# A transformer block's three step lists in another order: maxima bunched, weight tests spread over the first batch, next tokens fetched at other places

## The reference

```
qkv = x @ Wqkv + bqkv                     # 256 -> 768, 16 heads of 16
att = softmax(where(causal, q @ k^T / 4, -inf))
x   = layernorm(x + (att @ v) @ Wout + bout)
h   = silu(x @ W1^T * s1) * (x @ W2^T * s2)   # 256 -> 1024
h   = gelu(h @ H1^T * sh1)                    # 1024 -> 1024, exact gelu
h   = gelu(h @ H2^T * sh2)                    # 1024 -> 1024
out = layernorm(x + h @ W3^T * s3)            # 1024 -> 256
```

## Time and profile before

| | |
|---|---|
| median of 3 runs | 2191.09 us (2189.73 to 2191.16) |
| profiled execution | 2188.74 us, span 2187.0 us |
| TensorE (PE) | 2129.8 us busy, 97% |
| VectorE (DVE) | 1248.7 us, 57% |
| ScalarE (ACT) | 1317.0 us, 60% |
| GpSimd (POOL) | 489.7 us, 22% |
| mean granted TensorE clock | 0.990 |
| first 140 us | iteration 0 (first `max` at 16.5 us, weight flag at 140.7 us) |

### The profile page before, as it was taken

The page is one execution under the profiler, slowest core; times in us unless marked ns, Lnnn a source line. Parts: engine busy times, 40 slices in busy tenths (PEclk is TensorE's granted clock), DMA queues, the critical chain, the costliest instruction groups (busy, mean ns, idle before and its releaser), DMA issues.

```text
span 2187.0 us, 52042 instructions
## 1 busy us (share of the span) xinstructions
PE 2129.8 (97%) x16294; PEld 1873.9 (86%) x16294; DVE 1248.7 (57%) x3928; ACT 1317.0 (60%) x2807; POOL 489.7 (22%) x899
## 2 busy tenths in 40 slices
...
DMA packets 95941, 167.71 MB, mean 77 GB/s; under 512 B 19204, under 2 KB 38404, under 8 KB 95672
## 3 DMA queue, kind: packets, MB, share of 16 engines
...
...
## 4 chain that ended last, share of the span: by engine, by line
PE 88%; issue 1%; ACT 1%; SPq 1%; DVE 1%; DMA 1%; POOL 0%; ACTq 0%; DVEq 0%; POOLq 0%
PE ring L1236 44%; PE ring L1221 11%; PE pM L1111 7%; PE pS L1099 6%; PE pO L1159 6%; PE ring L1249 5%; PE ring L1171 4%; PE ring L1201 2%; PE ring L1191 2%; ACT probs_a L766 1%; PE ring L1143 1%; SPq L606 0%; DMA Qs<-nm 0%; PE ring L1210 0%; DMA rec<-rec_d 0%
## 5 line engine op out<-in xcount | busy, mean ns | idle before, releaser
L916 DVE CUSTOM_DVE_ANT_0 pM<-pM,mask 128x512 f32<-128x512 f32 (+3 forms) x1024 | 497.8, 502 | 361.6 <-PE pM L1111 298.9
L1236 PE MATMUL ring<-Yhi,H 128*128 128x256 f32 x1984 | 501.8, 290 | 0.3 <-DVE c L932 0.3
L1236 PE MATMUL ring<-Xhi,H 128*128 128x256 f32 x1984 | 497.7, 289 | 0.0
L1236 PE MATMUL ring<-Ylo,H 128*128 128x256 f32 x1984 | 487.4, 282 | 0.0
L1236 PE MATMUL ring<-Xlo,H 128*128 128x256 f32 x1984 | 486.1, 282 | 0.0
L1236 PEld LDWEIGHTS ring<-Yhi,H 128*128 128x128 f32 x1984 | 377.1, 190 | 10.6 <-issue 6.5
L1236 PEld LDWEIGHTS ring<-Ylo,H 128*128 128x128 f32 x1984 | 378.0, 190 | 6.8 <-issue 3.3
L1236 PEld LDWEIGHTS ring<-Xlo,H 128*128 128x128 f32 x1984 | 379.3, 191 | 1.4
L1236 PEld LDWEIGHTS ring<-Xhi,H 128*128 128x128 f32 x1984 | 378.4, 191 | 1.5 <-issue 0.2
L1111 PE MATMUL pM<-Ks,Qs 128*128 128x512 f32 x992 | 301.1, 343 | 16.1 <-DVE mx L916 9.4
L860 ACT ACTIVATE Yhi<-ring,cols 128x256 fp32r<-128x256 f32 x248 | 117.1, 472 | 277.3 <-PE ring L1236 155.8
...
## 6 DMA issues: line engine op xcount, KB each, us to landing
qk_d<-c SPq DMA_DIRECT2D x120, 256.0 KB, 3.4
Qs<-qk_d SPq DMA_DIRECT2D x120, 192.0 KB
Ks<-qk_d SPq DMA_DIRECT2D x120, 192.0 KB
qk_d<-c SPq DMA_DIRECT2D x120, 128.0 KB, 3.1
...
raw<-in_h ACTq DMA_DIRECT2D x8, 1024.0 KB, 11.4
H<-raw ACTq DMA_DIRECT2D x8, 1024.0 KB, 10.0
```

Source lines behind the costliest of these rows:

```text
L916: nc.vector.tensor_tensor_reduce(pM[:, h % 2, 0:n], pM[:, h % 2, 0:n], mask[:, T - n:T], 1.0, NEG, ALU.add, ALU.max, mx[:, t, h:h + 1]).th ...
L1236: mm = nc.tensor.matmul(to, w, x_part, start=(k == 0 and m == 0), stop=(k == KB - 1 and m == 1))
```

## The change

The three lists `ORDER`, `HEAD_ORDER` and `FIRST_ORDER` are written in another order. The steps are the same, except that a few go from `FIRST_ORDER` to `HEAD_ORDER` or `ORDER` and back; `TAIL_ORDER` and all code stay. Line numbers grow by 5. All lists change throughout; of the diff these lines hold what is spoken of later:

```
 ORDER = """
...
-h_act:-2:h2:1:7 h_rest:-2:h2:1:7 h2:-2:1:7:0 h2:-2:1:7:1 x1_turn:-1:0 max:0:2:3:0 ffn_out:-2:1:0 ffn_out:-2:1:1
-table:0:Exp:2 exp:0:1:0 exp:0:1:1 max:0:2:3:1 x1_turn:-1:1 exp:0:1:2 exp:0:1:3 max:0:2:3:2 exp:0:1:4 max:0:2:3:3
-exp:0:1:5 gu:-1:0:0 exp:0:1:6 gu:-1:0:1 exp:0:1:7 ffn_hi:-1:0:0 gu:-1:0:2 exp:0:1:8 ffn_hi:-1:0:1 max:0:2:2:0
...
+h_rest:-2:h2:1:6 h2:-2:1:6:1 h2:-2:1:7:0 h2:-2:1:7:1 max:0:2:3:1 h_rest:-2:h2:1:7 x1_turn:-1:0 table:0:Exp:2
+ffn_out:-2:1:0 x1_turn:-1:1 exp:0:1:0 exp:0:1:1 ffn_out:-2:1:1 exp:0:1:2 max:0:2:3:2 exp:0:1:3 gu:-1:0:0
+exp:0:1:4 max:0:2:3:3 exp:0:1:5 gu:-1:0:1 exp:0:1:6 ffn_hi:-1:0:0 gu:-1:0:2 max:0:2:2:0 exp:0:1:7 ffn_hi:-1:0:1
...
-h2:-1:0:7:0 h_rest:-1:h2:0:5 h2:-1:0:7:1 neg_max:0:3 h_rest:-1:h2:0:6 h_rest:-1:h2:0:7 qk:1:1 ffn_out:-1:0:0
-table:0:Exp:6 ffn_out:-1:0:1 exp:0:3:0 exp:0:3:1 gu:-1:1:0 exp:0:3:2 gu:-1:1:1 exp:0:3:3 max:1:0:3:0
...
+h2:-1:0:6:1 h_rest:-1:h2:0:5 h_rest:-1:h2:0:6 h_rest:-1:h2:0:7 h2:-1:0:7:0 neg_max:0:3 h_act:-1:h2:0:7
+h2:-1:0:7:1 max:1:0:3:0 qk:1:1 ffn_out:-1:0:0 table:0:Exp:6 exp:0:3:0 max:1:0:3:1 exp:0:3:1 stack:1:1
...
 HEAD_ORDER = """
...
-exp:0:3:8 weight_test:0:1 exp:0:3:9 exp:0:3:10 weight_test:0:2 weight_test:0:3 weight_test:0:4 weights:0:8
...
+exp:1:0:1 max:1:1:3:3 max:1:1:2:0 raw:0:10 exp:1:0:2 exp:1:0:3 max:1:1:2:1 exp:1:0:4 weight_test:0:9 den_turn:0
+max:1:1:2:2 exp:1:0:5 max:1:1:2:3 exp:1:0:6 exp:1:0:7 qk:1:2 exp:1:0:8 exp:1:0:9 stack:1:2 y:0:0:0 max:1:1:1:0
+max:1:1:1:1 y:0:0:1 exp:1:0:10 y:0:1:0 max:1:1:1:2 max:1:1:1:3 y:0:1:1 max:1:1:0:0 max:1:1:0:1 ln1_stats:0
+weights:0:10 max:1:1:0:2 max:1:1:0:3 neg_split:1:1 pv:1:0:1 neg_max:1:1 weight_test:0:10 ln1:0 low_bits:0 qk:1:3
...
```

More of the change, by code:

```diff
@@ L62 @@
 ORDER = """
[L63 to L67, removed]
@@ L83 @@
[L83 to L87, removed]
@@ L93 @@
[L93 to L97, removed]
@@ new lines @@
+exp:0:0:7 exp:0:0:8 max:0:1:2:1 max:0:1:2:2 h2:-2:1:1:0 exp:0:0:9 exp:0:0:10 h2:-2:1:1:1 table:0:Gelu:1
+max:0:1:2:3 h2:-2:1:2:0 h_rest:-2:h2:1:0 h_act:-2:h2:1:0 max:0:1:1:0 pv:0:0:1 max:0:1:1:1 h2:-2:1:2:1
+max:0:1:1:2 h_rest:-2:h2:1:1 max:0:1:1:3 h2:-2:1:3:0 max:0:1:0:0 h2:-2:1:3:1 h_rest:-2:h2:1:2 max:0:1:0:1
+h2:-2:1:4:0 max:0:1:0:2 max:0:1:0:3 h_act:-2:h2:1:1 h_act:-2:h2:1:2 h_act:-2:h2:1:3 h_act:-2:h2:1:4 ln1_stats:-1
+h2:-2:1:4:1 h_rest:-2:h2:1:3 neg_split:0:1 ln1:-1 qk:0:3 h_act:-2:h2:1:5 h2:-2:1:5:0 h2:-2:1:5:1 h2:-2:1:6:0
@@ new lines @@
+h2:-1:0:7:1 max:1:0:3:0 qk:1:1 ffn_out:-1:0:0 table:0:Exp:6 exp:0:3:0 max:1:0:3:1 exp:0:3:1 stack:1:1
+ffn_out:-1:0:1 gu:-1:1:0 exp:0:3:2 gu:-1:1:1 ffn_hi:-1:1:0 exp:0:3:3 gu:-1:1:2 exp:0:3:4 ffn_hi:-1:1:1
+max:1:0:3:2 gu:-1:1:3 exp:0:3:5 ffn_hi:-1:1:2 gu:-1:1:4 exp:0:3:6 ffn_hi:-1:1:3 max:1:0:3:3 exp:0:3:7 gu:-1:1:5
+max:1:0:2:0 ffn_hi:-1:1:4 exp:0:3:8 gu:-1:1:6 ffn_hi:-1:1:5 gu:-1:1:7 exp:0:3:9 max:1:0:2:1 exp:0:3:10
+ffn_hi:-1:1:6 table:0:Gelu:7 h1:-1:1:0:0 ffn_hi:-1:1:7 pv:0:3:1 v:1:0 max:1:0:2:2 max:1:0:2:3 h_rest:-1:h1:1:0
@@ L101 @@
+h1:-1:1:6:1 h1:-1:1:7:0 neg_max:1:0 den_turn:0 h_rest:-1:h1:1:7 h1:-1:1:7:1 h_act:-1:h1:1:7 qk:1:2 v:1:3
 """
 HEAD_ORDER = """
[L105 to L108, removed]
@@ L114 @@
-max:0:2:1:0 max:0:2:1:1 exp:0:1:5 exp:0:1:6 max:0:2:1:2 weights:0:4 weights:0:5 max:0:2:1:3 pv:0:1:0 max:0:2:0:0
-max:0:2:0:1 weight_test:0:0 raw:0:8 qk:1:0 exp:0:1:7 exp:0:1:8 max:0:2:0:2 max:0:2:0:3 exp:0:1:9 neg_split:0:2
-max:0:3:3:0 weights:0:6 exp:0:1:10 neg_max:0:2 max:0:3:3:1 weights:0:7 pv:0:1:1 max:0:3:3:2 exp:0:2:0 exp:0:2:1
-max:0:3:3:3 max:0:3:2:0 exp:0:2:2 max:0:3:2:1 exp:0:2:3 max:0:3:2:2 max:0:3:2:3 exp:0:2:4 max:0:3:1:0
-max:0:3:1:1 o_out:0:1 max:0:3:1:2 exp:0:2:5 exp:0:2:6 max:0:3:1:3 max:0:3:0:0 exp:0:2:7 raw:0:9 stack:1:0
@@ L129 @@
-o_out:1:0 max:1:1:0:0 pv:1:0:1 max:1:1:0:1 max:1:1:0:2 max:1:1:0:3 neg_max:1:1 ln1_stats:0 neg_split:1:1 ln1:0
-qk:1:3 exp:1:1:0 max:1:2:3:0 max:1:2:3:1 exp:1:1:1 x1_turn:0:0 exp:1:1:2
+load_x:0 raw:0:0 qk:0:0 raw:0:1 qk:0:1 columns:0 v:0:0 stack:0:0 qk:0:2 max:0:0:3:0 max:0:0:3:1 raw:0:2
+stack:0:1 max:0:0:3:2 max:0:0:3:3 max:0:0:2:0 weights:0:0 max:0:0:2:1 weights:0:1 max:0:0:2:2 max:0:0:2:3 qk:0:3
+raw:0:3 max:0:0:1:0 max:0:0:1:1 stack:0:2 raw:0:4 max:0:0:1:2 max:0:0:1:3 max:0:0:0:0 max:0:0:0:1 stack:0:3
```

107 lines of the change are left out of this document (61 added, 46 removed).

## The result

The changed kernel takes 2171.57 us, median of 4 runs (2170.3 to 2173.73), against 2190.56 for the kernel before in the same comparison (2189.73 to 2191.16): ratio 0.9915, 95% interval 0.9897 to 0.9932. The forecast was 2173, between 2160 and 2190. The total is right; two of its terms are not, and they work against each other.

What follows compares the result with a forecast made beforehand. The prediction took TensorE to bound the loop's iterations, and VectorE with the chain through ScalarE the first batch. From 2188.7 us it took 14 (loop) and 4 (first batch), then added 2.4 for the median: 2173 us, range 2160 to 2190.

Steps and rivals of the forecast that it cites:

- The loop, 1.0 us an iteration: Iterations 2 to 15, softmax of group 1: 1.36 - 0.16 - 0.2 = 1.0 us gained each, 14 us.
- the ring of score buffers: Group 1: each score matmul needs the exponential of the one two before; 1.04 us lost per iteration, which would go.
- The 0.32 ahead of the first score matmul: Group 1: TensorE waits 0.32 us for the negated maxima, issued behind the saves of qk:0:3; half, 0.16, left standing.
- the 0.2 charged for groups 0 and 3: Per iteration: negated maxima's copy for group 3, behind a Gelu pair on ScalarE, might come late; 0.2 us charged.
- this room (4.8 us): TensorE work covering the negated maxima's chain, 4.86 us for group 0 and 4.8 for group 3, against 4.6 needed.
- The first batch, 4 us: First batch: half of VectorE's 8.07 us idle stretch behind six weight tests taken as gained, 4 us.
- the two causes I named: First batch: six weight tests in a row, holding GpSimd's selects, and the next batch's maxima starting late; stake 14.8 us.
- The last weights, counted at nothing: First batch: last piece of weights fetched late, VectorE waiting 6.5 us at worst; counted at nothing.
- Iteration 15 like the others: Iteration 15 was counted with iterations 2 to 14, each gaining 1.0 us.
- the whole stake: Rival: loop and first batch gain all their loss, 19 + 14.8 us, giving 2157 us; chance 0.12.
- that ORDER does nothing: Rival: no gain in the iteration, only the first batch's 4 us, giving 2187 us; chance 0.10.
- the negated maxima of groups 0 and 3: Rival: these wait on ScalarE behind Gelu pairs, 2.4 us per iteration against 1.36 gained, giving 2202 us; chance 0.10.

Runs made afterwards that it cites:

- e10: The changed kernel with group 1's output transfer behind the negated maxima, and group 1's first two score matmuls and second x1_turn put back behind the second half of ffn_out: 2181.29 us.
- e3: The kernel before with only group 1's place in ORDER changed: second x1_turn and first two score matmuls ahead of the second half of ffn_out; 2217.24 us.
- e2: The kernel before with only the two lists of the first batch (HEAD_ORDER, FIRST_ORDER) new: 2177.55 us, ratio 0.9950.
- e7: The kernel before with three weight tests moved in HEAD_ORDER, so that three stand in a row instead of six: 2192.84 us.
- e12: The kernel before with weight tests spread, qk:1:1 and five maxima early, then tests 7 to 10, two v and low_bits moved in HEAD_ORDER as well: 2188.48 us.
- e1: The kernel before with only the list of the iteration (ORDER) new and the first batch's lists old: 2177.68 us, ratio 0.9952.

## Why the prediction was right, and where it was not

- *The loop, 1.0 us an iteration*: right in size (1.04 over twelve iterations) and in place (e10), and for the stated reason: the loss between the first score matmul of group 1 and `gu`, put down to the ring of score buffers at 1.04 us, was 1.03 and fell to 0.08, and the waits for the exponentials fell from 22 places to 4. Two small terms were off and cancelled. The 0.32 ahead of the first score matmul was read from iteration 6 alone; over the loop it was 0.13 before and 0.16 after, so nothing was gained there instead of 0.16. And the 0.2 charged for groups 0 and 3 was not paid: no wait for their negated maxima shows. That it came out at 1.04 so closely is luck to that extent.
- *The gain as a property of a few steps*: too simple. e3 shows that the new order of the place costs 27 us where the negated maxima are not copied sooner. I had measured this room (4.8 us) for groups 0 and 3 and not asked what the second half of `ffn_out` had covered in group 1.
- *The first batch, 4 us*: the term that was mis-sized. It is 9.5 at the flag and 7.8 at batch 2 in the trace, and 11 by e2. I took half of one idle stretch of VectorE; the lists shorten more than that one, and e7 to e12 show that the two causes I named do not give it by themselves.
- *The last weights, counted at nothing*: VectorE waited 2.2 us, inside the bound of 6.5, and TensorE 2.2 with it. It was named as a sign that the forecast is wrong; it was paid for out of a gain larger than forecast.
- *Iteration 15 like the others*: wrong. 2.5 us were lost behind batch 14, where the sum has 1.0 gained, 3.5 apart. The forecast gave the issues of a moved step no cost: the output of group 1 issues five transfers, and with these ahead of the negated maxima the pause of SyncE fell between the maxima's own. e4, which moves the output back behind them, gets 4.4 us of this piece back (211.3 us); of the 5.8 us between the medians of after and e4 the rest is no more than the first batch differs by from trace to trace (flag at 131.16 and 129.12 us). Nothing in the waits of before showed that pause, since it fell where nobody waited; the timeline of SyncE's issues did (2016.77 above).
- *No cost for the stack loads, the token fetch, `h_rest`*: right in the loop, no new wait names them.
- *Rivals*: the whole stake was not gained (7.8 to 11 of 14.8 in the first batch); that ORDER does nothing is excluded by e1; the negated maxima of groups 0 and 3 were never waited for.

Without the pause the forecast would have been 7 us too high (e4: 2165.81). The miss in the first batch, 11 instead of 4, and the one in iteration 15, 5.8 us between the medians of after and e4, work against each other.
